# Cosine attention in a two-layer transformer kernel: values held still in TensorE, squared scores streamed

## The reference, cut to what matters

```python
queries, keys, values = (l2norm(queries), l2norm(keys), l2norm(values))
sim  = einsum('bhid,bhjd->bhij', queries, keys)
attn = square(relu(sim))
aggr = einsum('bhij,bhjd->bhid', attn, values)
n    = norm(aggr, axis=-1)                       # over the 64 dimensions of a head
out  = tanh(n) * (aggr / maximum(n, EPS)) * tanh(silu(gates))
x    = x + out.reshape(b, n, h * d) @ Wout
```

## Time and profile before

| what | value |
|---|---|
| device time, median of 3 runs | 1991.81 us |
| lowest and highest of them | 1962.36 and 2462.54 us |
| the profiled execution's own span | 2019.7 us |
| busy over that span | PE 72%, DVE 61%, POOL 47%, ACT 37% |
| chain that ended last, by engine | PE 45%, DVE 25%, time in which nothing shown was waited for 10%, POOL 8%, ACT 5% |
| costliest group of the page | L1117, the aggregates: 293.2 us |

### The profile page before, as it was taken

How to read it: one execution, slowest core, us unless ns; L and a number is a source line. 1 busy time by engine, 2 the same in 40 slices (tenths; PEclk the granted TensorE clock), 3 DMA queues, 4 the chain that set the end, 5 groups by cost and what they waited for, 6 DMA issues and landing times.

```text
span 2019.7 us, 28317 instructions
## 1 busy us (share of the span) xinstructions
PE 1449.9 (72%) x8634; PEld 933.4 (46%) x8635; DVE 1233.7 (61%) x2840; ACT 750.5 (37%) x1206; POOL 949.0 (47%) x1080
## 2 busy tenths in 40 slices
PE   3434326478787878778878872899989989984876
PEld 2222214146665656566666671334333333334765
DVE  6877841387876777778778742565746556553332
ACT  1101002144444444444444430445544454541221
POOL 2346476466665656566666442131312213124554
PEclk7555555578887878888888875777876687786777
DMA  4000006100000000000000003000000000001110
GB/s 123 22 24 14 12 7 127 43 5 7 8 8 1 6 6 6 6 6 6 6 6 9 3 3 94 6 9 17 14 10 8 16 8 16 5 11 37 43 42 12
DMA packets 73355, 40.91 MB, mean 20 GB/s; under 512 B 23811, under 2 KB 68716, under 8 KB 73284
## 3 DMA queue, kind: packets, MB, share of 16 engines
q1 hardware_dynamic: 50530, 24.02, 4.3%
q0 software_dynamic: 20384, 11.67, 2.9%
q10 hardware_dynamic: 2370, 4.35, 0.8%
HBM read 31.11 MB, written 23.87 MB: 27 GB/s over the span
## 4 chain that ended last, share of the span: by engine, by line
PE 45%; DVE 25%; issue 10%; POOL 8%; ACT 5%; another core or an unknown queue 3%; DMA 2%; ACTq 1%; POOLq 1%; SPq 0%; DVEq 0%
PE psum L1117 8%; PE psum L1221 6%; PE psum L1242 5%; PE psum L1168 4%; DVE o L1581 3%; PE psum L1251 3%; PE psum L1211 2%; PE psum L1154 2%; POOL yg L631 2%; POOL out L753 2%; PE psum L1126 2%; PE psum L1145 1%; PE psum L1283 1%; DVE rden L1433 1%
## 5 line engine op out<-in xcount | busy, mean ns | idle before, releaser
L1117 PE MATMUL psum<-v,attn 128*128 128x64 f32 x2048 | 293.2, 304 | 25.6 <-ACT aggr L846 17.1
L1117 PEld LDWEIGHTS psum<-v,attn 128*128 128x128 f32 x2048 | 277.2, 217 | 61.9 <-issue 45.7
L1741 DVE TENSOR_REDUCE terms<-psum 128x2 bf16<-128x512 f32 x256 | 170.2, 692 | 94.8 <-PE psum L1242 87.0
L683 POOL TENSOR_SCALAR veps<-meanvar 128x2 f32<-128x2 f32 x32 | 6.1, 192 | 423.4 <-DVE meanvar L1719 423.4
L921 ACT ACTIVATE prob<-psum 128x512 f32<-128x512 f32 x256 | 143.6, 597 | 100.8 <-PE psum L1211 98.6
L1221 PE MATMUL psum<-prob,v 128*32 128x256 f32 x1024 | 172.2, 466 | 0.8 <-ACT pvT L926 0.8
L631 POOL DMA_INDIRECT yg<-ye_dram,routel x128 | 142.1, 1110 | 59.8 <-issue 37.3
L560 POOL DMA_INDIRECT xe_dram<-rows_out,route x128 | 130.9, 1023 | 39.7 <-issue 39.4
L1242 PE MATMUL psum<-k_highT,q_highT 32*128 32x256 bf16 x512 | 127.7, 344 | 29.7 <-DVE terms L1741 27.0
L1126 PE MATMUL psum<-ident,o 128*128 128x128 f32 x256 | 50.1, 360 | 118.8 <-DVE silu_g L1675 82.1
L831 ACT ACTIVATE attn<-psum 128x1024 f32<-128x1024 f32 x128 | 130.1, 1017 | 14.0 <-PE psum L1100 11.2
(11 more groups left out here) (300 smaller groups left out, 3088.7 us busy)
## 6 DMA issues: line engine op xcount, KB each, us to landing
x4n_dram<-x4n SPq DMA_DIRECT2D x16, 256.0 KB, 2.2
w<-in_w POOLq DMA_DIRECT2D x48, 64.0 KB, 2.7
x_in<-in_x SPq DMA_DIRECT2D x8, 256.0 KB, 2.9
xe_dram<-zero_rows SPq DMA_DIRECT2D x8, 256.0 KB, 3.3
x_dram<-x1s SPq DMA_DIRECT2D x8, 256.0 KB
xe_dram<-rows_out,route POOLq DMA_INDIRECT x128
xe<-xe_dram SPq DMA_DIRECT2D x16, 128.0 KB
ye_dram<-ye SPq DMA_DIRECT2D x16, 128.0 KB, 2.2
```

Source lines behind the costliest of these rows:

```text
L1117: mm = pe.matmul(psum[:, 4 + j, (head % HALF) * DV:(head % HALF + 1) * DV], attn[g % RING][:, h, c * SEQ + j * P:c * SEQ + (j + 1) * P], v ...
L1741: dve.tensor_reduce(terms4[:, 0, j, head:head + 2, 6, 0], bank[4 + a2].rearrange("q (b k) -> q b k", b=2), AX, ALU.max, negate=True).then_ ...
```

## The change

- In `aggregate` the operands change places. The values of one head (128 keys by 64) are the weights, and the squared scores (256 queries) are streamed. The two heads of a pair write partitions 0 to 63 and 64 to 127 of one bank, in turn. The aggregate so comes out with (head, dimension) on partitions and queries along the free axis, which is what W wants; `turn_oT`, `take_oT` and the copy to `aggr` go.
- The gates are projected transposed as well (two products of 256 columns in place of one of 512).
- ACT squares the aggregate straight from PSUM (`square_aggregate`, two instructions for a half). The sum over 64 partitions goes through PE: the squares are the weights, and a two-column mask `half_of` is streamed (`norms_of`, eight fp32 products for a half). DVE copies 16 columns (`take_norm`).
- POOL no longer scales gates. It splits the factor into three bf16 terms (`split_factor`, five instructions on 128x16). PE turns these (`turn_factors`, two transposes), ACT copies them (`take_factors`, 24x256), and PE spreads them over the 64 partitions of each head with a constant (`spread`, four bf16 products for a half).
- DVE multiplies aggregate (PSUM) and gates (`gate_aggregate`, two instructions of 128x512 for a half) early, and the result with the spread factors (PSUM) late (`scale_output`, two more).
- The squares of pairs 4 and 5 move from DVE to ACT (`square_attention`).
- W moves from g = 6 to g = 7, behind the first query and key transposes. In `half`, the new pieces take these places: on PE `turn_factors(tail, 0)` at the end of g = 1, `spread(tail, 0)` and `norms_of(tail, 1)` at the end of g = 2, `turn_factors(tail, 1)` at g = 5, `spread(tail, 1)` at g = 6, `norms_of(att, 0)` at g = 6 after the aggregate of pair 4 and ahead of the transposes.
- Two small constants are loaded at the start.

```diff
+        POOL_PAIRS = (2, 3, 6)
+        ACT_PAIRS = (4, 5)
+        DVE_PAIRS = (0, 1, 7)
 ...
+            def split_factor(q, hf):                       # POOL
+                m = 2 * (q.n - 1) + hf + 1
+                hold(s["o_tanh_made"], m)
+                hold(s["factorT_ps"], m - 1)
 ...
                 if tail:
                     length_of(tail, 1)
                 if att:
                     square(att, POOL_PAIRS[0])
                 if tail:
-                    scale_gate(tail, 1)
+                    split_factor(tail, 1)
                 if att:
                     square(att, POOL_PAIRS[1])
 ...
+            def take_factors(q, hf, x):                    # ACT
+                wait(act, s["spread_ps"], 2 * (2 * (q.n - 1) + hf))
+                act.wait_ge(s["factorT_ps"], 2 * (q.n - 1) + hf + 1)
+                act.activation(factorT[:], ring[x].bitcast(BF16)[0:FROWS, 0:SEQ], ACT.Copy).then_inc(s["factorT_made"], 1)
 ...
                     if att:
                         relu(att, g)
+                    if tail and g == 5:
+                        take_factors(tail, 1, 1)
+                    if att and g in ACT_PAIRS:
+                        square_attention(att, g)
 ...
+                    if tail and g == 4:
                         tanh_of_norm(tail, 1)
 ...
             def aggregate(q, g):                           # PE
-                hf = g // 4
-                if g % 4 == 0:
-                    wait(pe, s["aggr_out"], 2 * (q.n - 1) + hf)
+                m = 2 * (q.n - 1) + g // 4
+                if g % 2 == 0:
+                    wait(pe, s["gated_made"], 2 * (m - 1) + g % 4 // 2 + 1)
 ...
+                for c in range(2):
                     for h in range(2):
                         head = 2 * g + h
+                        mm = pe.matmul(psum[DV * h:DV * h + DV, 4 + g % 4 // 2, g % 2 * SEQ:(g % 2 + 1) * SEQ], v[q.p][:, c, head * DV:(head + 1) * DV],
+                                       attn[g % RING][:, h, c * SEQ:(c + 1) * SEQ], start=(c == 0), stop=(c == 1))
 ...
+            def norms_of(q, hf, x):
+                m = 2 * (q.n - 1) + hf + 1
+                b = fill(x, [(s["o_norm_made"], m)], [(s["aggr_sq_made"], 2 * m)])
+                for i in range(HALF // 2):
+                    for j in range(2):
+                        mm = pe.matmul(b[:, HALF * j + 2 * i:HALF * j + 2 * i + 2], aggr_sq[:, i // 2, i % 2 * SEQ + j * P:i % 2 * SEQ + (j + 1) * P], half_of[:], start=True, stop=True)
+                mm.then_inc(s["norm_ps"], 1)
+            def turn_factors(q, hf, x):
+                m = 2 * (q.n - 1) + hf + 1
+                b16 = fill(x, [(s["factorT_made"], m)], [(s["factor_terms_made"], m)]).bitcast(BF16)
 ...
+            def spread(q, hf):
+                m = 2 * (q.n - 1) + hf
+                for i2, x in ((0, 1), (1, 0)):
+                    b = fill(x, [(s["o_made"], 2 * m + i2 + 1)], [(s["factorT_made"], m + 1)])
 ...
                             dve.tensor_copy(v[front.p][:, g - 1, 512 * h:512 * h + 512], ring[1 - h][:]).then_inc(s["v_copied"], 1)
+                            if tail and k == 0:
+                                gate_aggregate(tail, 1)
 ...
+                    if tail and g == 2:
+                        scale_output(tail, 0)
+                        take_norm(tail, 1, 1)
 ...
                     if front and g == 5:
                         split_terms(front)
                     if att and g == 5:
-                        norm_of(att, 0)
+                        gate_aggregate(att, 0)
                     if fetch and g == 5:
                         combine(fetch)
                     if tail and g == 6:
+                        scale_output(tail, 1)
+                    if att and g == 6:
+                        take_norm(att, 0, 0)
+                    if tail and g == 7:
                         wait(dve, s["x3_stored"][tail.p], 16 * (tail.k - 1))
                         dve.wait_ge(s["y3_ps"], tail.n)
```

More of the change, by code:

```diff
@@ L29 @@
 TERMS = 4
+FTERMS = 3
+FROWS = FTERMS * HALF
 DH = 8
@@ L874, in half @@
                             square_of(front, 2 + 2 * (g - 1) + h, v[front.p][:, g - 1, 512 * h:512 * h + 512])
+                    if tail and g == 1:
+                        take_factors(tail, 0, 1)
                     if front and g in (3, 4):
@@ L1140, in half @@
                         scores(att, g)
+                    if tail and g == 6:
+                        spread(tail, 1)
+                    if tail and g == 7:
+                        b = fill(1, [(s["x3_made"], tail.n)], [(s["o_made"], 4 * tail.n)])
+                        for j in range(2):
+                            for c in range(PAIRS):
+                                mm = pe.matmul(b[:, j * D:(j + 1) * D], oT[:, c, j * P:(j + 1) * P], w_out[:, c, :], start=(c == 0), stop=(c == PAIRS - 1))
+                        mm.then_inc(s["y3_ps"], 1)
                     if front and g == 0:
@@ L1147, in half @@
                         aggregate(tail, 6 + g)
+                    if tail and g == 5:
+                        turn_factors(tail, 1, 1)
                     if att and g >= 2:
@@ L1637, in half @@
                         square(tail, PAIRS - 1)
-                    if g > 0 and att and g - 1 not in POOL_PAIRS:
+                    if g > 0 and att and g - 1 in DVE_PAIRS:
                         square(att, g - 1)
@@ L1699, in half @@
                         normalise3(fetch)
-                    if att and g == 7:
-                        gated_output(att, 0)
                 chain.restart()
```

175 lines of the change are left out of this document (85 added, 90 removed).

## The result

The changed kernel takes 2047.6 us (median of 5 runs, 2039.3 to 2087.7), the kernel before beside it 1986.2 us (median of 5). The ratio is 1.034, with a 95% interval of 1.025 to 1.043: slower by some 61 us. The direction held, and so did the chain of waits in the second half of the step; the holds by POOL and the clock came out otherwise. The size was 52 us too large, and most of that, in this trace, lies in how the kernel before was read, not the changed one.

The account below looks back on a forecast made before the run. The step was taken as a chain passing from engine to engine: 51.2 us with holds plus 5.3 of clock gave 56.5, 8.3 above 48.2; 13 steps made 108 us, thus 2100 us against the median, range 1980 to 2150.

Parts of the forecast that it names:

- the chain of waits in the second half of the step: PE waits 2.8 us for pair 2, 4 for factors, 3.7 for pair 4, 4.3 for the norms' ring bank.
- First half: Step start to inverse roots at full clock: aggregate savings spent on new waits; DVE reaches roots at t = 20.6, against 20.1.
- POOL's holds: POOL's late squares of pairs 2 and 3 hold DVE's inverse roots: first instruction 1.6 us, Newton steps 1.9 us.
- Second half: Factor turn at t = 29.1, then copies, split, products, `combine`, scalings; norms of `att` at 40.1, step 51.2 us at full clock.
- The clock at the end of the step: PE's waits bring half clock: norms +1.8, transposes +1.0, W +2.5 us, together 5.3 us a step.
- A sign that failed: Among the signs that would show the forecast: PE busy less, below 36 us a step.
- The base: Step of the kernel before, from 15 intervals between sums of L1693: 48.2 us, subtracted from 56.5 and multiplied over 13 steps.
- The aggregates: On PE, two heads run at once in alternating array halves: a pair about 0.85 us, 1.0 less, 8 us a step.
- PE as the bound: Rival: PE's waits stay, 5 us of work vanish; 43.2 us a step, 1927 us; chance 0.14.
- No holds: Rival: POOL holds nothing on the roots, clock still falls; 53.2 us a step, 2057 us; chance 0.18 with one-hold case.
- Clock stays full: Rival: PE's clock does not fall, POOL's holds are there; 51.2 us a step, 2031 us; chance 0.07.
- The two heads do not run at once: Rival on PE's aggregates: 0.85 us more on pairs 6, 7, 1 and 5, 3.4 a step, 2144 us; chance 0.07.

Follow-up runs that it names:

- `high` first: Changed kernel with ACT making `high` ahead of `take_factors` and the square of pair 5: 2073.1 us, ratio 1.037 to the kernel before.
- the roots first: Changed kernel with DVE's inverse roots ahead of the first two silu products: 2031.0 us, ratio 1.027 to the kernel before.
- the run with PE kept busy: Changed kernel with seven unread fp32 products a step put on PE in its waits: 2040.8 us, ratio 1.035 to the kernel before.
- the fastest kernel: Changed kernel with `high` earlier, POOL's scaling of v later, `combine` behind the last scaling, inverse roots ahead of silu products: 1956.6 us, ratio 0.987.

## Why the prediction was right, and where it was not

**The step, right to 1 us, by errors that cancel.** Forecast 56.5, measured 55.6. DVE reached the roots 3.1 us later than forecast, the holds cost 1.9 less, and the clock at the end 0.7 to 2.2 less: that these meet within 1 us is luck. The times below are those of the step shown, a longer one.
- *First half.* The start of v was put at t = 4.2 and came at 4.9, the third v product at 10.1 and came at 10.2, waiting for the factor copy as foreseen. The norms were put at 14.2 to 16.3 and ran 13.9 to 17.1: their start is right, their end is not. The clock was taken as full there; it falls to half at 958.4, so the norms take 3.20 us instead of 1.9 and the gates 2.81 instead of 1.99. The roots start at t = 23.7 instead of 20.6. In about every second step these norms keep the full clock almost to their end (the short ones are near 2.1 us), and with that the steps alternate between 55.8 and 56.8.
- *POOL's holds.* Forecast 1.6 on the first root instruction and 1.9 on the Newton steps, 3.5 in all. Measured: because DVE was late as well, POOL's square of pair 2 had ended before the roots began (967.1 against 967.74), and the square of pair 3 fell on the scaling behind them, 1.6 us. The mechanism holds wherever the two overlap (each reordering of POOL, of the roots or of `high` above shows it); what failed is the assumption that POOL is late and DVE is not.
- *Second half.* The factor turn was put at 29.1 and came at 30.5; the norms at 40.1 and came at 41.4. Each length between them agrees within 0.5 us. The wait for the norms' bank has the last scaling as its releaser and `combine` just before it, as written down. Taking `combine` away from there gave back 3.3 of its 3.4 us.
- *The clock at the end of the step.* Forecast +1.8 on the norms, +1.0 on the transposes, W at 6.16. Measured 3.57 (+1.7), 1.89 (+0.8 over the 1.07 of the last transposes) and W between 4.3 and 5.8. The term was 5.3 and is 3.1 to 4.6. The reason given, the long waits, is not shown: with most of those waits filled the clock still fell, inside the norms, and the rests of the waits remain as a rival.
- *A sign that failed.* PE was to be busy below 36 us a step. It is busy 42.0 us in the step shown (941.05 to 997.84), where one of the kernel before has 40.7 (959.69 to 1009.74): the clock is 0.76 over the one and 0.86 over the other.

**The base, wrong: 48.2 us.** The step of the kernel before was taken as 723.3 / 15. Two of the 15 intervals are the ones that drain the pipeline, 39.9 and 27.2 us. The other 13, which stand for the steps that the sum multiplied by, have a mean of 50.5; the step that the prediction walked through lasts 49.25 by its own rows (965.85 to 1015.10). So 13 x 8.3 = 108 should have been 13 x (56.5 - 50.5) = 78; with the measured step it is 13 x (55.6 - 50.5) = 66. The drain, put at nothing, is 6.9 us shorter after (36.5 and 23.7 us), and 66 - 6.9 is the 59.3 that the first row shows. The way from there to the 61 us between the medians is the first sum, 7.3 us earlier, and other stages. In this trace the one division accounts for 30 of the 52 us by which the forecast was too long.

Three of those 13 steps before are 54 to 56 us long. Each has a wait like this one on DVE, and on ACT beside it, at the place where other steps wait for the aggregates on PE; the profile does not know its releaser:

```profile
616.37 0.69 DVE L1615 TENSOR_REDUCE norm<-squares 128x32 f32<-128x512 f32 x1 [6.24 <-remote]
```

Without them the mean step before is 49.1. They occur in no other profile here; what they are stays open. If a usual execution of the kernel before has none, the change costs 6.4 us a step and not 5.1, and the division only some 12 us of the forecast (13 x 0.9): estimates, which no profile here can settle.

**The aggregates, right in size, wrong in mechanism.** A pair was put at 0.85 us alone and takes 1.08 to 1.09, 0.8 less than the 1.89 of before where 1.0 was forecast. The reason given, two heads that run at once by turning between the halves of the array, is refuted: without the turns the pair takes the same time. The row that seemed to speak for it, L1221 with no gain, was read as if at full clock. It was at half:

```profile
1504.60:1506.70 2.10, 2.10 (x11) 0.75 (x10) 0.00 (x0) 1.05 (x2) 0.00 (x0) 0.50 0.00 0
```

Its 1.93 us for 8 records would be near 1.0 at full clock (an estimate, half of it), which is about what the new form costs. Read with its clock, that row alone would have given the size.

**The rivals.** PE as the bound (1927 us) is refuted by the waits: four of the five stand about where forecast, and DVE and POOL lost 92 and 51 us of work for nothing. "No holds" (2057 by the same wrong base) is half true, as one hold of 1.6 us is left. "Clock stays full" is refuted by the windows. "The two heads do not run at once" put a pair at 1.7 us; it takes 1.08.

## What to carry to other kernels

Take a step's length from the intervals of the steps that the sum will multiply, not from the stage divided by their number. When work moves off an engine, walk every queue and look for the instruction that now stands alone between a producer and its consumer: here one reordering of two lines (`combine` behind the scaling) was worth 3.3 us of a step. And before an operation is moved earlier, look at what the other engine of DVE and POOL does at the new time: `high` first and the roots first gave most of their gain to a hold, and got it back only when POOL's long instruction went elsewhere.

## What the runs showed of the hardware that was not expected

- Four fp32 products (eight records) of 256 columns past 64-wide weights take 1.08 us at full clock, whether two heads alternate between the halves of the array or follow each other (1.09). Past 128-wide weights they take 1.99.
- The clock can fall when PE is busy again, after an idle stretch that it came through at 1.00: 0.9 us behind the wait of 3.94 us in the changed kernel, 0.7 us behind the rest of 2.13 us in the run with PE kept busy, and 0.4 us into the norms of the tail, behind gaps of 1.63, 0.80 and 0.28 us. It then stayed at 0.50 with PE busy 3.00 of 3.00 us (959.3 to 962.3). Which of the gaps or the work brings it down is not shown.
- POOL's elementwise products hold more of DVE than the gated product: a Newton step (0.26 to 1.83 us), the scaling (1.22 to 2.80), the split into fp16 (1.23 to 3.69), and instructions with one tensor from SBUF, the first of the roots (0.20 to 1.96) and the normalised x (0.34 to 3.65). Beside the same instructions of POOL, instructions with one of two inputs from PSUM kept their lengths: the silu product beside the scaling of v at 973.83 (two in 1.27 us) and, in the fastest kernel, the sum of a sequence (0.42 at most). The Trainium skill, page "SBUF — State Buffer", section "Who interferes with whom", counts copies, casts and tensor_scalar among the DVE instructions that can take the pair of ports that it shares with GpSimd; the two rows with one input, both tensor_scalar, agree.
- The hold goes both ways: POOL's scaling of v takes 3.62 us where it starts with nothing of DVE beside it (roots first, at 968.68), and 4.60 in the changed kernel, where it starts at 972.79 beside DVE's scaling of queries and keys, which runs to 973.90.
